# Constants behind x, masks read straight from PSUM, half of the fold inside the first pass, weight loads on three queues

## The reference

```python
z = einsum('bchw,oc->bohw', x, rot_w) + rot_b          # 3 forms a pixel
z = batchnorm(z)                                       # over all 8 images
angle = tanh(sum_over_forms(mean_hw(z))) * pi / 4      # one angle an image
phase = exp(-2j * pi * cos(angle) * fsum)              # 27 frequencies
w2d = ifftn(w_fft * phase).real[:, :, :, mid]          # 3x3 taps, one set an image
out = conv2d(x_image, w2d_of_image, padding=1)
# layer 0: x = x + conv(groupnorm(x));  layer 1: the same with fixed weights, circular
```

## Time and profile before

| | |
|---|---|
| time, median of 3 runs | 1781.84 us (1781.26 to 1783.27) |
| the profiled execution's own time | 1781.29 us |
| its span, first to last instruction | 1779.5 us, so 1.8 us lie around it |
| busy in the span | PE 1647.2, DVE 1386.7, ACT 1169.5, POOL 128.1 us |
| first pass, by VectorE's chunks | 12.4 to 330.2 us |
| chain to the first convolution | 330.2 to 362.0 us |
| convolutions | 362.0 us to the end |

### The profile page before, as it was taken

The page is one execution under the profiler, slowest core; times in us unless marked ns, Lnnn a source line. Parts: engine busy times, 40 slices in busy tenths (PEclk is TensorE's granted clock), DMA queues, the critical chain, the costliest instruction groups (busy, mean ns, idle before and its releaser), DMA issues.

```text
span 1779.5 us, 65074 instructions
## 1 busy us (share of the span) xinstructions
PE 1647.2 (93%) x29275; PEld 1245.5 (70%) x29275; DVE 1386.7 (78%) x2175; ACT 1169.5 (66%) x1044; POOL 128.1 (7%) x361
## 2 busy tenths in 40 slices
PE   5887888577789999999999999999999999999899
PEld 5787787433356667887788668866886678666655
DVE  6989999689877887878878888788888788777500
ACT  6888788568666666666666666666666666666344
POOL 0000000030120010002000200020002001100100
PEclk9999999789899999999999999999999999999999
DMA  9999999454446565656665665565656655655245
GB/s 386 422 422 422 421 422 422 171 160 152 130 160 206 196 210 179 227 195 203 211 210 191 206 209 202 205 200 202 213 186 205 213 197 198 215 193 194 96 196 202
DMA packets 101781, 411.55 MB, mean 231 GB/s; under 512 B 16883, under 2 KB 19496, under 8 KB 85160
## 3 DMA queue, kind: packets, MB, share of 16 engines
q1 hardware_dynamic: 100744, 407.81, 63.2%
q0 software_dynamic: 800, 0.15, 0.1%
HBM read 271.82 MB, written 136.07 MB: 229 GB/s over the span
## 4 chain that ended last, share of the span: by engine, by line
PE 68%; DVE 16%; DMA 6%; issue 5%; ACT 2%; POOL 1%; SPq 1%; DVEq 0%; ACTq 0%; POOLq 0%
PE ps L406 35%; PE ps L399 31%; DVE x L633 6%; DMA x<-x_pix 6%; DVE nat L682 3%; DVE x L846 3%; DVE stats L884 1%; ACT x L473 1%; ACT nat L498 1%; PE ps L350 0%; ACT x L513 0%; PE ps L351 0%; SPq L248 0%; PE ps L358 0%; SPq L285 0%
## 5 line engine op out<-in xcount | busy, mean ns | idle before, releaser
L399 PE MATMUL ps<-nat,wc 64*64 64x512 f16 x12480 | 1169.5, 378 | 36.4 <-DVE nat L682 14.7
L406 PE MATMUL ps<-x,wc 64*64 64x512 f16 (+2 forms) x12585 | 1161.3, 375 | 13.9 <-POOL x L613 13.9
L399 PEld LDWEIGHTS ps<-nat,wc 64*64 64x64 f16 x12480 | 666.0, 107 | 231.8 <-issue 26.0
L406 PEld LDWEIGHTS ps<-x,wc 64*64 64x64 f16 x12585 | 676.4, 107 | 194.5 <-POOL x L613 17.7
L498 ACT ACTIVATE nat<-xin,gnp 128x1024 f16<-128x1024 f32 (+1 forms) x264 | 299.8, 1137 | 307.4 <-PE ps L399 296.6
L846 DVE SCALAR_TENSOR_TENSOR x<-ps,gnp,x 128x1024 f16<-128x1024 f32 (+1 forms) x264 | 333.0, 1262 | 28.0 <-ACT x L513 20.8
L528 ACT ACTIVATE outb<-ps,bias 128x1024 f32<-128x1024 f32 (+1 forms) x264 | 289.4, 1096 | 80.1 <-PE ps L406 63.9
L682 DVE SCALAR_TENSOR_TENSOR nat<-xin,gnp,nat 128x1024 f16<-128x1024 f32 (+1 forms) x264 | 332.4, 1260 | 2.0 <-ACT nat L498 1.9
L517 ACT ACTIVATE x<-ps,gnp 128x1024 f16<-128x1024 f32 (+1 forms) x231 | 252.9, 1095 | 113.0 <-DVE stats L884 112.5
L350 PE MATMUL ps<-x 128*128 128x129 f16 x2048 | 256.2, 225 | 60.7 <-DVE x L633 60.6
L633 DVE SCALAR_TENSOR_TENSOR x<-x 128x2048 bf16<-128x2048 f32 x128 | 284.1, 2285 | 17.4 <-ACT x L473 15.7
(11 more groups left out here) (125 smaller groups left out, 263.3 us busy)
## 6 DMA issues: line engine op xcount, KB each, us to landing
x<-x_pix SPq DMA_DIRECT2D x128, 1024.0 KB, 13.5
xin<-x_tiles SPq DMA_DIRECT2D x256, 512.0 KB, 3.7
out<-outb SPq DMA_DIRECT2D x256, 512.0 KB, 4.1
xin<-x_tiles SPq DMA_DIRECT2D x8, 192.5 KB, 2.5
out<-outb SPq DMA_DIRECT2D x8, 192.5 KB, 3.3
w<-taps_scratch SPq DMA_DIRECT2D x64, 8.0 KB, 1.7
w<-taps_scratch SPq DMA_DIRECT2D x28, 16.0 KB, 2.6
taps_scratch<-x POOLq DMA_DIRECT2D x21, 3.0 KB, 3.3
```

The lines of the kernel that those rows point to most:

```text
L399: return nc.tensor.matmul(ps[64 * kind:64 * kind + 64, bank, 0:w], lhs, nat[rows, xhl, a:a + w], start=first, stop=last)
L406: ins = nc.tensor.matmul(ps[64 * kind:64 * kind + 64, bank, done:done + part], lhs, x1[rows, xhl, z:z + part], start=first and done == 0, ...
```

## The change

- SP sends x first. Four of the constants (`firsts`, `rotw`, `small`, `wf`) go on ACT's queue; `consts` and `w1band` follow the first four chunks of `x_tiles` on SP, under a semaphore of their own, `late_in`, for which TensorE waits ahead of the moments' product.
- An image is taken out of PSUM by four operations with no waits between them: for each bank the product with the mask straight from PSUM, and the column scaled. `gmask` and `colsum` keep both banks; the fold adds them with a second matrix `fold2`, twice `fold`.
- The fold of images 0 to 3 and its reduction go inside the first pass, ahead of the last pair of images. The column sums' product is no longer ahead of the reduction.
- `zpad` is zeroed at the very start, so that SP can zero the scratch tensor as soon as its queue comes to it.
- Of the eight weight loads on SP four go to ACT, after hi0 of chunks 0 and 1. VectorE's `weights0` stands after lo0 of chunks 0 and 1, ahead of those of 2 and 3.
- Early tiles are laid out anew: `tapsb` before `gmask` (TAPS_SLOT is now 32 and not 35), and `alo` and `ahi` start at other addresses.

```diff
@@ sync
-            for dst, src in ((cst[:, :], consts), (first, firsts), (rw[:, :], rotw), (smallp[:, :], small),
-                             (wfs, wf), (w132[:, :], w1band)):
-                sp.dma_start(dst, src).then_inc(const_in, 16)
@@
             for g in range(NX):
                 load_x(g)
+            for dst, src in ((cst[:, :], consts), (w132[:, :], w1band)):
+                sp.dma_start(dst, src).then_inc(late_in, 16)
 
             hold(sp, zve, Z_ZPAD)
...
-            load_weights(sp, 0, ((1, 0), (1, 1)), w_in)
+            load_weights(sp, 0, ((1, 0),), w_in)
@@ tensor
+            def fold(h):
+
+                pe.wait_ge(a_mask, 4 * (4 * h + 4 + 2))
+                for f, name in enumerate(("fold", "fold2")):
+                    m = nc.tensor.matmul(ps[0:C, 6 + h, 0:512], c(name),
+                                         gmask[:, f, 4 * h:4 * h + 4, :].rearrange("p b q -> p (b q)"),
+                                         start=f == 0, stop=f == 1)
+                m.then_inc(folded, 1)
+
+            with pe.Fori(0, B // 2 - 1) as bb:
+                gram_pair(bb)
+            pe.wait_ge(const_in, 16 * 4)
+            fold(0)
+            with pe.Fori(B // 2 - 1, B // 2) as bb:
+                gram_pair(bb)
...
-            pe.wait_ge(zve, Z_SUMS)
-            for h in range(2):
-                mm(ps[0:C, 2 + h, 0:512], c("fold"), gmask[:, 4 * h:4 * h + 4, :].rearrange("p b q -> p (b q)"), False)
-            mm(ps[0:C, 4, 0:B], c("fold"), colsum)
+            fold(1)
+            for f in range(2):
+                m = nc.tensor.matmul(ps[0:C, 4, 0:B], c("fold"), colsum[:, f, :], start=f == 0, stop=f == 1)
+            m.then_inc(folded, 1)
+            pe.wait_ge(late_in, 16 * 2)
@@ scalar
+            for dst, src in ((first, firsts), (rw[:, :], rotw), (smallp[:, :], small), (wfs, wf)):
+                act.dma_start(dst, src).then_inc(const_in, 16)
...
-            for g in range(NX):
+            for g in range(2):
+                hi0(g)
+            act.wait_ge(zdma, 16 * 4)
+            load_weights(act, 0, ((1, 1),), w_in)
+            for g in range(2, NX):
                 hi0(g)
@@ vector
-                    V.tensor_copy(gtmp, ps[:, h, 0:P]).then_inc(a_part, 1)
-                    V.tensor_copy(gcol[:, 0:1], ps[:, h, P:P + 1]).then_inc(a_part, 1)
-                    ve.wait_ge(a_part, 3 * b + 2)
-                    V.scalar_tensor_tensor(gtmp, ps[:, 2 + h, 0:P], 2.0, gtmp, ALU.mult, ALU.add).then_inc(a_part, 1)
-                    V.tensor_tensor(colsum[:, bass.ds(b, 1)], ps[:, 2 + h, P:P + 1], gcol[:, 0:1], ALU.add)
-                    hold(ve, a_part, 3 * b + 3)
-                    V.tensor_tensor(gmask[:, bass.ds(b, 1), :].rearrange("p b q -> p (b q)"), gtmp,
-                                    c("mask_g"), ALU.mult).then_inc(a_mask, 1)
+                    for f in range(2):
+                        V.tensor_tensor(gmask[:, f, bass.ds(b, 1), :].rearrange("p b q -> p (b q)"), ps[:, 2 * f + h, 0:P],
+                                        c("mask_g"), ALU.mult).then_inc(a_mask, 1)
+                        V.tensor_scalar(colsum[:, f, bass.ds(b, 1)], ps[:, 2 * f + h, P:P + 1], AS, None, ALU.mult
+                                        ).then_inc(a_mask, 1)
+
+            def fold_sums(h):
+
+                ve.wait_ge(folded, h + 1)
+                return V.tensor_reduce(gram[:, 4 * h:4 * h + 4, :],
+                                       ps[0:C, 6 + h, :].rearrange("p (b k c) -> p b c k", b=4, k=8),
+                                       AX.X, ALU.add)
+
+            with ve.Fori(0, B // 2 - 1) as bb:
+                halves_pair(bb)
+            fold_sums(0).then_inc(zve, 1)
+            with ve.Fori(B // 2 - 1, B // 2) as bb:
+                halves_pair(bb)
...
-            for g in range(NX):
+            for g in range(2):
                 lo0(g)
             for part in range(4):
                 weights0(0, part)
+            for g in range(2, NX):
+                lo0(g)
```

More of the change, by code:

```diff
@@ L83 @@
 _COLS = [("gm", 128), ("id0", 256), ("id1", 256), ("pmask", 2), ("row0", 1), ("rown", 1)]
-_FIRST = [("mask_g", 128), ("fold", 16), ("rep", 128), ("pair", 16), ("id16", 16),
+_FIRST = [("mask_g", 128), ("fold", 16), ("fold2", 16), ("rep", 128), ("pair", 16), ("id16", 16),
           ("ones", 128), ("u", 9), ("v", 9), ("trig", 4), ("quarter", 1), ("image", 8)]
@@ L160, in conv_program @@
         apix = early(ASLOTS * ACHUNK).rearrange("p (s n) -> p s n", s=ASLOTS)
-        gmask = early(B * P).rearrange("p (b q) -> p b q", b=B)
-        colsum, gcol, gtmp = early(B), early(1), early(P)
+        assert at_[0] + 256 <= NCH * CH // 2
+        TAPS_AT = at_[0]
+        tapsb = early(256, 9 * B)
+        gmask = early(2 * B * P).rearrange("p (f b q) -> p f b q", f=2, b=B)
+        colsum = early(2 * B).rearrange("p (f b) -> p f b", f=2)
         gram = early(B * C, C).rearrange("p (b c) -> p b c", b=B)
         zpad = early(400)
-        tapsb = early(256, 9 * B)
-        TAPS_AT = at_[0]
         early(at_[0] % 2)
@@ L175, in conv_program @@
         assert at_[0] <= RCOLS
-        TAPS_SLOT = min((TAPS_AT - 256) // (CH // 2), RING - 1)
+        TAPS_SLOT = TAPS_AT // (CH // 2)
         def c(name, parts=P):
@@ L185, in conv_program @@
         const_in = sem("const_in")
+        late_in = sem("late_in")
+        folded = sem("folded")
         a_in = [sem(f"a_in{s}") for s in range(ASLOTS)]
@@ L190, in conv_program @@
         a_zero = sem("a_zero")
-        a_part = sem("a_part")
         a_mask = sem("a_mask")
@@ L244, in load_weights @@
             for half, r in groups:
[L245 to L250, removed]
+                g = (half * 2 + r) * 2 * C
+                for row, count, m in ((r, 4, 0),) if half == 0 else ((2 + r, 2, 0), (r, 2, 128)):
+                    for ci in range(2):
+                        at_ = g + ci * C
+                        eng.dma_start(w32[at_:at_ + C, m:m + 64 * count].rearrange("c (a m) -> c a m", m=64),
+                                      taps[b, :, row:row + count, ci:ci + 4, :].rearrange("c a q o -> c a (q o)")
+                                      ).then_inc(signal, 16)
         def reads(n):
@@ L335, in _, with gram_pair @@
             pe.wait_ge(a_zero, 1)
-            with pe.Fori(0, B // 2) as bb:
+            def gram_pair(bb):
                 for h in range(2):
@@ L341, in _ @@
                     accs = [ps[:, 2 * part + h, 0:P + 1] for part in range(2)]
-                    pe.wait_ge(a_mask, b + 1)
+                    pe.wait_ge(a_mask, 4 * b + 4)
                     for acc in accs:
@@ L360, in mm @@
                     m.then_inc(zpe, 1)
-            pe.wait_ge(const_in, 16 * 6)
-            pe.wait_ge(zve, Z_SUMS)
-            for h in range(2):
-                mm(ps[0:C, 2 + h, 0:512], c("fold"), gmask[:, 4 * h:4 * h + 4, :].rearrange("p b q -> p (b q)"), False)
-            mm(ps[0:C, 4, 0:B], c("fold"), colsum)
+            fold(1)
[3 more added lines that the diff above has]
+            pe.wait_ge(late_in, 16 * 2)
             pe.wait_ge(zve, Z_MOM)
@@ L621, in _, with halves_pair @@
             ve.sem_inc(a_lo, ASLOTS)
-            ve.sem_inc(a_mask, 2)
+            ve.sem_inc(a_mask, 8)
+            V.memset(zpad, 0.0).then_inc(zve, 1)
             V.memset(ahi[:, :, :, P:P + 1], 1.0)
             V.memset(zerof, 0.0).then_inc(a_zero, 1)
-            ve.wait_ge(const_in, 16 * 6)
-            with ve.Fori(0, B // 2) as bb:
+            ve.wait_ge(const_in, 16 * 4)
+            def halves_pair(bb):
                 for h in range(2):
@@ L688, in lo0 @@
                 ins.then_inc(lo0_ready, 1)
-            count = [0]
+            count = [2]
             def go(ins):
@@ L719, in at @@
                 assert k == n, (k, n)
-            link(V.memset(zpad, 0.0))
-            ve.wait_ge(a_mask, B + 2)
-            at(link(V.tensor_scalar(colsum, colsum, AS, None, ALU.mult)), Z_SUMS)
-            after_pe()
-            for hh in range(2):
-                n = go(V.tensor_reduce(gram[:, 4 * hh:4 * hh + 4, :],
-                                       ps[0:C, 2 + hh, :].rearrange("p (b k c) -> p b c k", b=4, k=8),
-                                       AX.X, ALU.add))
+            n = go(fold_sums(1))
+            ve.wait_ge(folded, 3)
             go(V.tensor_copy(zc[0:C, 0:8], ps[0:C, 4, 0:8]))
@@ L1045 @@
 Z_ZPAD = 1
-Z_SUMS = 2
-Z_MOM = Z_SUMS + 5
+Z_MOM = 2 + 4
 Z_VAR = Z_MOM + 4
@@ L1082, in constants @@
     put("fold", (ch[:, None] == np.arange(C)[None, :]) / (AS * AS * NPIX))
+    put("fold2", 2.0 * (ch[:, None] == np.arange(C)[None, :]) / (AS * AS * NPIX))
     put("gm", (ch[:, None] // GROUP == ch[None, :] // GROUP) / (8 * GROUP))
```

## The result

| | before | changed |
|---|---|---|
| median of 22 runs each | 1782.61 us (1780.84 to 1784.32) | 1779.30 us (1777.30 to 1783.21) |
| ratio | | 0.9982, 95% interval 0.9976 to 0.9988 |
| the profiled execution's span | 1779.5 us | 1777.5 us |

The change wins 3.3 us, between 2.1 and 4.3. That is a gain clear of noise, but under the 3.6 us (0.2%) that the prediction took as the bound of "faster": by its own line the result is "same", which it gave 0.31, and not "faster" with 0.64. The forecast was 1777.3 with a range of 1774.6 to 1780.6. Of 4.55 us forecast 3.3 came, and the parts did not come in the sizes that the sum gave them.

What follows compares the result with a forecast made beforehand. It saw a first pass with full DMA engines (VectorE a close second), a one-engine-at-a-time chain, then TensorE-bound convolutions. 2.2 - 0.3 + 1.15 + 0.5 + 0.6 + 0.4 = 4.55 us gave 1777.3 us, range 1774.6 to 1780.6.

Steps and rivals of the forecast that it cites:

- the six terms of the sum: Gains in us: x first 2.2, fold in pass -0.3, masks 1.15, shorter fold 0.5, single reduction 0.6, weights 0.4.
- rival A: At the weights: POOL's weight loads land behind x, losing 1.1 to 1.9 us; time 1779.2, chance 0.17.
- the three signs: Wrong if VectorE's 2.21 us moved, POOL's loads took over 3 us to land, or first convolution chunk exceeded 7.2 us.
- x first: At the start: x issued earlier, less a delay from constants sharing the DMA engines; gain 2.2 us.
- The step on the issue: At the start: with six issues gone from SP, x is issued near 1.45, 2.65 us earlier.
- Fold in the pass: Behind image 5: VectorE's stop grows from 4.38 to 5.65 us, mostly worked off by the pass's end; -0.3 us.
- the 0.45 of "issue": Behind image 5: last summand, 0.45 us, of VectorE's forecast 5.65 us stop, for its restart after the reduction.
- Rival B: At the pass's end: the fold makes VectorE the bound, its stop growing by 1.7 more; time 1779.0, chance 0.10.
- Masks, fold, reduction: From the pass's end to the moments: masks straight from PSUM 1.15, shorter fold 0.5, one reduction 0.6 us gained.
- The row: Pass's end: profile row with two operations without a wait 0.20 us apart, lasting 0.29; basis of the masks' 1.15 us.
- Weights: At the chain's end: loads on three queues, VectorE free earlier, POOL's last load landing in 2.5 us; gain 0.4 us.
- Rivals C and D: C: all covers hold, 1776.0, chance 0.12. D: VectorE, slower at new addresses, bounds the first pass, 1790.1, chance 0.05.

## Why the prediction was right, and where it was not

The time fell in the range, and five of the six terms of the sum came within 0.4 us of their sizes. The sixth, the weights, came with the other sign, by the mechanism of rival A, which had a chance of 0.17 and named 1779.2; 1779.3 was measured. That this is so near is in part luck, since 0.8 us of it are the base (below). Two of the three signs by which the prediction said that it would be wrong were seen: POOL's loads landed after 3.5 and 3.6 us (over 3), and the first chunk took 8.60 us (over 7.2).

**x first: 2.2 forecast, 1.8 in the mean.** The step on the issue held to 0.05 us (1.40). VectorE's last chunk began at 327.92, 328.10 and 328.65 in the three traces with the old start, 328.22 in the mean, and in the eight with the new at 327.44, 326.13, 325.88, 326.38, 326.06, 326.06, 325.95 and 327.33, 326.40 in the mean. (The last of the three old ones is the one with another order of constants; without it the difference is 1.6.) What I had not seen is that the start is not one number: in the two late ones the first chunk is used at 8.47 and 8.67, in the others at 6.5 to 7.2, with the same issue times up to the fourth. In those two SP's fourth issue took 0.90 and 1.03 us, in the others none over 0.42. Whether that is the cause was not tested. The first trace of the changed kernel is one of the two, so its 0.48 us stand for little.

**Fold in the pass: -0.3 forecast, 0 measured.** The stop grew by 0.66 and not by 1.27: VectorE starts again 0.6 us behind the reduction's start, so the 0.45 of "issue" that I added for the loop is not there, and TensorE has the four pieces ready 1.7 and not 1.95 us after the emptying begins. The fold of images 0 to 3 needs only their masks, so TensorE starts it at 251.58, before the emptying at 251.82. Rival B is excluded by every trace: the last chunk is x's in all of them.

**Masks, fold, reduction: 2.25 forecast, 2.5 measured.** The emptying gave 1.38 (2.05 to 0.67 us) for 1.15, the fold 0.52 for 0.5, the reduction 0.59 for 0.6. The row was the better basis: the four operations begin 0.21, 0.06 and 0.20 us apart and last 0.15 to 0.29. By the rule of the Trainium skill ("VectorE: DVE Perf Modes", section "The DRAIN you can't avoid") that leaving out semaphores saves nothing, I had 0.9 for it; the measurement is 1.38, so for operations this short the rule as I had applied it does not give the sum: none waits here for the one before it to end (the second begins 0.21 us behind the first, which lasts 0.29).

That 2.5 came is partly chance of the one trace of before. From emptying to moments it is 5.38, 5.81 and 6.64 us in the three traces with the old fold, by where TensorE's clock falls, and 3.31 or 3.32 in all eight that have the new one, whose products take 1.89 us each time. So the part is worth 2.1 to 3.3 us, 2.6 in the mean. The prediction took the clock's fall from one trace, as if it had a fixed place. The 0.18 us that the chain behind the moments was shorter in the first trace (15.66 us to the reciprocal, 15.84 before) are not the change's: the second trace of the changed kernel has 15.85.

**Weights: a gain of 0.4 forecast, a loss of 0.73 measured.** This is the step that failed, in sign. The mechanism is that of the prediction's own rival A: SP is free earlier, and 512 KB go beside POOL's last loads. I had weighed it with "more engines, only one load ahead", took 2.5 us for the landing, and it was 3.6; the rival's own 4.0 to 4.8 was too much, and the truth lay between. Holding chunk 4 gives 1.6 us back, which is the 0.7 lost and the 0.9 that the part was meant to win. The Trainium skill's rule that transfers of all issuers run on the same 16 DMA engines and interleave ("DMA: Bandwidth & Descriptors", section "Issuing engines are not separate DMA queues") fits the traces: held, chunk 4 of x leaves POOL's loads at 1.8 to 2.4 us, beside it they take up to 3.6.

**The sum and the base.** With the sizes found it is 1.8 + 2.5 - 0.7 = 3.6 us, against 3.3 measured (2.1 to 4.3), so there is no rest to explain. Of the 2.0 us between 1777.3 and 1779.3, 1.2 are the gain and 0.8 the base: the median before is 1782.61 over 22 runs and was 1781.84 over three. Landmarks of three traces, in us:

| | before | changed, first | changed, second |
|---|---|---|---|
| VectorE's last chunk begins at | 327.92 | 327.44 | 325.95 |
| emptying to moments | 5.81 | 3.32 | 3.31 |
| moments to the reciprocal | 15.84 | 15.66 | 15.85 |
| reciprocal to the weights | 5.57 | 6.30 | 6.30 |
| first chunk | 7.18 | 8.60 | 7.45 |
| from the first mask to the end | 1410.3 | 1409.3 | 1413.7 |

The last row is 1409.0 to 1411.3 us in all twelve traces but the second of the changed kernel. So what is won ahead of the first mask does reach the end, within some 2 us; that one trace lost 4.4 us against the first behind its first mask. The first chunk takes 7.18 us in the trace of before and 7.45 to 8.60 in the eight others read without the products of zeros, 7.93, 7.99 and 8.06 of them in the kernels with one part of the change alone. Nothing here shows that the change made it longer; whether the trace of before merely had a short one stays open. Rivals C and D are excluded: POOL's loads were late, and VectorE's chunk takes 35.29 / 16 = 2.21 us at the new addresses as at the old.

## What to carry to other kernels

When a queue is relieved, look at what it sends next, and at whose small transfers are then still on their way: here a cut of four issues made POOL's last load take 1.7 us longer to land, and one wait on SP won back more than the part was worth. When a chain of tiny steps precedes the main work, what stands at its end (the clock of TensorE, a row of transfer issues) costs as much as the steps themselves. And a part worth 1 or 2 us is read from landmarks within traces, since whole executions of one kernel differ by 1 to 6 us here; more than one trace is needed, since the landmarks move too (6.5 to 8.7 us at the start, 5.38 to 6.64 in the old fold).

## What the runs showed of the hardware

POOL's last two loads of 16 KB landed after 1.8 to 2.1 us in the six traces in which SP issued its load of 512 KB over 1 us later or held it, and after 3.4 to 3.7 us in the six in which SP issued it within 0.6 us of them (in the first trace of the changed kernel SP at 353.41, POOL at 353.48 and 353.98). Sixteen f32 products of 128x129 zeros, 5.98 us of TensorE's time, brought the clock from 0.50 (1.2 GHz) to 1.00 (2.4 GHz), where it stayed over a gap of 2.72 us; the next chunk took 4.79 us and not 7.2 to 8.6. The first use of x came between 6.5 and 8.7 us in kernels whose first four issues were at the same times. In the three traces with the old fold the clock fell from 1.00 to 0.50 at 333.5, 336.2 and 341.5 us, and the fold's row was 3.17, 2.34 and 1.91 us long; it began at 333.01, 334.87 and 335.04.
